# The shared expert's eight batches of a mixture-of-experts layer: next batch's tiles transposed earlier, the down product in two halves, scatters behind the subtractions, and 71 routed blocks in place of 72

## What is computed

```python
def _experts(x_flat, Wg, Wu, Wd):
    g = jax.nn.silu(jnp.einsum('nc,eci->nei', x_flat, Wg))
    u = jnp.einsum('nc,eci->nei', x_flat, Wu)
    return jnp.einsum('nei,eic->nec', g * u, Wd)

def _moe(x, Wgate, expert_bias, Wg, Wu, Wd, sWg, sWu, sWd):   # C = 512, E, K, I, S = 8, 2, 256, 1
    xf = x.reshape(-1, c)
    shared = jnp.mean(_experts(xf, sWg, sWu, sWd), axis=1)
    probs = jax.nn.softmax(xf @ Wgate + expert_bias, axis=-1)
    topk_p, topk_i = jax.lax.top_k(probs, K)
    topk_p = topk_p / jnp.sum(topk_p, axis=-1, keepdims=True)
    comb = jnp.sum(jax.nn.one_hot(topk_i, E, dtype=xf.dtype) * topk_p[..., None], axis=1)
    routed = jnp.einsum('ne,nec->nc', comb, _experts(xf, Wg, Wu, Wd))
    return (shared + routed).reshape(b, t, c)

# in the layer: xn = _rmsnorm(x, w_ln2); return x + _moe(xn, ...)
# around it:    x = x + tanh(g_ffn[0]) * layer(layernorm(x), ...)
```

## Time and profile before

| | us |
|---|---|
| median of 3 runs (lowest, highest) | 2361.26 (2359.19, 2361.65) |
| the profiled execution, its own time | 2359.61 |
| its span, first to last instruction | 2357.6 |
| start of the shared expert's first product on PE | 1792.18 |
| start of the routed stage's first block on PE | 2001.05 |

### The profile page before, as it was taken

The page is one execution under the profiler, slowest core; times in us unless marked ns, Lnnn a source line. Parts: engine busy times, 40 slices in busy tenths (PEclk is TensorE's granted clock), DMA queues, the critical chain, the costliest instruction groups (busy, mean ns, idle before and its releaser), DMA issues. The chain is left out here.

```text
span 2357.6 us, 43584 instructions
## 1 busy us (share of the span) xinstructions
PE 2130.3 (90%) x12672; PEld 972.2 (41%) x12673; DVE 1505.5 (64%) x4218; ACT 1177.9 (50%) x2316; POOL 1364.2 (58%) x1452
## 2 busy tenths in 40 slices
PE   3899999999999968899999999999976787999997
PEld 1333333333333313444444444444433343455554
DVE  3688888888888873656656656565535587344443
ACT  3355555555555543354545445454436473455553
POOL 3267767767767764265656565565451664455554
PEclk7999999999999978999999999999997898999999
DMA  5413323232332233453434435353314675666665
GB/s 172 156 56 107 95 90 108 77 113 70 107 104 76 85 101 94 139 151 95 141 119 134 129 96 161 89 155 120 102 50 118 132 179 106 110 112 113 115 108 88
DMA packets 222851, 263.78 MB, mean 112 GB/s; under 512 B 39192, under 2 KB 165004, under 8 KB 222388
## 3 DMA queue, kind: packets, MB, share of 16 engines
q1 hardware_dynamic: 197612, 212.79, 30.2%
q0 software_dynamic: 22976, 48.38, 11.9%
q10 hardware_dynamic: 2072, 0.28, 0.1%
HBM read 162.12 MB, written 86.80 MB: 106 GB/s over the span
## 5 line engine op out<-in xcount | busy, mean ns | idle before, releaser
L501 ACT ACTIVATE a_pt<-a_bank 128x512 f32<-128x512 f32 x512 | 305.6, 597 | 371.5 <-DVE a_bank L608 368.3
L1412 DVE CUSTOM_DVE_ANT_0 b_bank<-b_bank,b_tri 128x256 f32<-128x256 f32 (+3 forms) x512 | 253.6, 497 | 302.9 <-PE b_bank L1555 298.6
L619 DVE CUSTOM_DVE_ANT_0 a_bank<-a_bank,a_strip 128x512 f32<-128x512 f32 x512 | 353.1, 690 | 4.9 <-PE a_bank L762 4.3
L411 POOL TENSOR_TENSOR a_acc<-a_acc,a_pt 128x512 f32<-128x512 f32 x256 | 317.4, 1270 | 16.2 <-ACT a_pt L501 15.7
L1193 POOL TENSOR_TENSOR b_acc<-b_acc,b_pt 128x256 f32<-128x256 f32 (+2 forms) x384 | 270.9, 725 | 90.6 <-ACT b_pt L1284 71.3
L608 DVE TENSOR_TENSOR a_bank<-a_bank,a_band 128x256 f32<-128x256 f32 (+1 forms) x512 | 205.6, 402 | 129.6 <-PE a_bank L749 128.4
L1284 ACT ACTIVATE b_pt<-b_bank 128x256 f32<-128x256 f32 (+2 forms) x384 | 143.8, 383 | 190.9 <-PE b_bank L1539 181.0
L749 PE MATMUL a_bank<-a_q_stack,a_k_stack 128*128 128x512 f16 x512 | 199.3, 390 | 22.7 <-ACT a_pt L501 14.0
L762 PE MATMUL a_bank<-a_k_stack,a_q_stack 97*128 97x512 f16 x512 | 196.4, 384 | 4.6 <-DVE a_low L619 4.5
L1933 POOL DMA_INDIRECT out_dram<-c_z,c_to_row x72 | 114.1, 1585 | 138.7 <-DMA out_dram<-c_z,c_to_row 101.8
L408 POOL TENSOR_TENSOR a_acc<-a_pt 128x512 f32<-128x512 f32 x128 | 159.9, 1270 | 4.9 <-ACT a_pt L501 4.9
(11 more groups left out here) (346 smaller groups left out, 5432.3 us busy)
## 6 DMA issues: line engine op xcount, KB each, us to landing
b_q_stack<-qk_rows SPq DMA_DIRECT2D x192, 128.0 KB, 2.6
a_q_stack<-qk_rows SPq DMA_DIRECT2D x96, 128.0 KB
a_k_stack<-qk_rows SPq DMA_DIRECT2D x96, 128.0 KB
b_k_stack<-qk_rows SPq DMA_DIRECT2D x96, 128.0 KB, 2.6
a_sums<-in_x SPq DMA_DIRECT2D x34, 256.0 KB, 3.1
qk_rows<-a_qk_hi SPq DMA_DIRECT2D x64, 128.0 KB, 1.7
qk_rows<-a_qk_lo SPq DMA_DIRECT2D x64, 128.0 KB, 1.8
out_dram<-a_sums SPq DMA_DIRECT2D x32, 256.0 KB, 2.0
```

What stands on the lines that cost most here:

```text
L411: nc.gpsimd.tensor_tensor(acc[:, hh, :], acc[:, hh, :], mine, ALU.add).then_inc(pooled, 1)
L501: nc.scalar.activation(pt[:, n % SLOTS, :], st_bank[n % 2][:], ACT.Exp).then_inc(exped, 1)
L619: nc.vector.tensor_tensor_reduce(out=max_bank[step % 2][:], in0=max_bank[step % 2][:], in1=strip[:, g * HG + hh, at:at + S], scale=-1.0, s ...
L1412: nc.vector.tensor_tensor_reduce(out=max_bank[step % 2][:, 0:w], in0=max_bank[step % 2][:, 0:w], in1=tri[:, at:at + w], scale=-1.0, scalar ...
```

## The change

It has five parts.

1. The next batch's tiles are transposed in the first half of a batch (tiles 0 and 1 after the first of the four up products, 2 and 3 after the second), and the copies and subtractions that go with them move too. On ACT, `square(b + 2)` now stands between the two halves, ahead of `squash(b, 1)`, and `normalise(b + 2)` at the end of the batch.
2. The down product is done in two halves: for tiles 0 to 2 first half 0 of the contraction, then half 1, then tile 3 whole. The first half waits for the low part of hidden half 0 only.
3. On POOL the scatters are dealt out by an iterator over (batch, tile): they may lag by up to a batch, and fewer of them stand between the two subtractions. `rms(b + 2)` now stands ahead of the second subtraction. The buffers `place_i` and `record` and the semaphore `scattered` are threefold in place of twofold.
4. On DVE, `choose(b + 1)` comes ahead of the weights' last part, and in the last batch `lay_blocks` stands ahead of the second `activate`.
5. `NB` is 71 in place of 72 (the most blocks that the ceilings of eight counts with the sum 64 x 128 can need), so the loop has 15 turns and more blocks are written out behind it.

```diff
-NB = 2 * TT + E
+NB = 2 * TT + E - 1
...
-            for j in range(NB - 4, NB + 1):
+            for j in range(NB - 4 - NB % 4, NB + 1):
                 call(Count(0, j, 4))
...
+            tiles = iter(itertools.product(range(B), range(NT)))
+            left = [B * NT]
+
+            def scatter_some(b, n):
+                for _ in range(min(n, left[0] - (B - 1 - b) * NT)):
+                    scatter(*next(tiles))
+                    left[0] -= 1
...
                 if b > 1:
-                    scatter(b, (0,))
+                    scatter_some(b, 2)
                 low_part(b, 0)
-                if b == 1:
-                    scatter(0, (0, 1))
-                elif b:
-                    scatter(b, (1, 2))
-                low_part(b, 1)
-                if b == 1:
-                    scatter(0, (2, 3))
-                elif b:
-                    scatter(b, (3,))
+                if b > 1:
+                    scatter_some(b, 1)
                 if b + 2 < B:
                     rms(b + 2)
-                if b == 1:
-                    scatter(1, range(NT))
+                low_part(b, 1)
+                if b:
+                    scatter_some(b, 2 if b > 1 else NT)
...
                 squash(b, 0)
                 if more:
                     high(b + 1, 0)
                     high(b + 1, 1)
+                    scale_gate(b + 1, range(0, 2))
+                    high(b + 1, 2)
+                    high(b + 1, 3)
                 hidden_high(b, 0)
-                if more:
-                    scale_gate(b + 1, range(0, 2))
+                if b + 2 < B:
+                    square(b + 2)
                 squash(b, 1)
                 if more:
-                    high(b + 1, 2)
-                    high(b + 1, 3)
+                    scale_gate(b + 1, range(2, 4))
                 hidden_high(b, 1)
-                if more:
-                    scale_gate(b + 1, range(2, 4))
                 if b + 2 < B:
-                    square(b + 2)
+                    normalise(b + 2)
                 if more:
                     exponential(b + 1)
                 weights(b + 1)
...
-                activate(b, 0)
-                if not more:
-                    lay_starts()
-                    low_part(0)
                 if more:
                     low(b + 1, 0)
                     low(b + 1, 1)
+                else:
+                    lay_starts()
+                activate(b, 0)
+                if more:
+                    low(b + 1, 2)
+                    low(b + 1, 3)
+                else:
+                    low_part(0)
+                    lay_blocks()
                 if b:
                     up_weights(b)
                 activate(b, 1)
...
-                for t in range(NT):
-                    down(b, t)
+                for t in range(NT - 1):
+                    down(b, t, (0,))
+                for t in range(NT - 1):
+                    down(b, t, (1,))
+                down(b, NT - 1, (0, 1))
```

More of the change, by code:

```diff
@@ L1745, in pass_c @@
             sem(n) for n in ("logits_done", "routed", "expd", "chosen_set", "ranked", "placed", "weighed", "recorded"))
-        scattered = [sem(f"scattered{i}") for i in range(2)]
+        scattered = [sem(f"scattered{i}") for i in range(3)]
         ranks_read, spare_found, blank_set, blanked, table_ready = (
@@ L1823, in _, with enter @@
             sp.wait_ge(table_ready, 1)
-            for i in range(2):
-                sp.wait_ge(scattered[i], 16 * 2 * NT * (B // 2))
+            for i in range(3):
+                sp.wait_ge(scattered[i], 16 * 2 * NT * ((B - i + 2) // 3))
+            def enter(j, u, use):
+                sp.wait_ge(entered[u], use * 16 + 16)
+                sp.nop(nofuse=True)
+                at = sp.value_load(block_i[0:1, 1, bass.ds(j, 1)], min_val=0, max_val=E * CAP + (E - 1) * P)
+                sp.dma_start(entry[:, bass.ds(j, 1), :].rearrange("p a f -> p (a f)"), table[bass.ds(at, P), :]).then_inc(entered[u], 16)
             with sp.Fori(0, NB // 4) as i:
                 for u in range(4):
[L1828 to L1832, removed]
+                    enter(i * 4 + u, u, i)
+            for j in range(NB // 4 * 4, NB):
+                enter(j, j % 4, j // 4)
             for i in range(3):
@@ L1862, in write_records, with scatter @@
                                       ).then_inc(recorded, 1)
-            def scatter(b, tiles):
-                s = b % 2
-                if b == 0:
+            def scatter(b, t):
+                s = b % 3
+                if (b, t) == (0, 0):
                     pool.wait_ge(blanked, 32)
[L1868 to L1873, removed]
+                if t == 0:
+                    pool.wait_ge(weighed, b + 1)
+                    pool.wait_ge(recorded, 2 * b + 2)
+                for c in range(2):
+                    pool.indirect_dma_start(table, bass.IndirectOffsetOnAxis(place_i[:, s, t, c:c + 1], 0), record[:, s, t, c, :], None
+                                            ).then_inc(scattered[s], 16)
+            tiles = iter(itertools.product(range(B), range(NT)))
[4 more added lines that the diff above has]
+                    left[0] -= 1
             nc.gpsimd.memset(ones[:], 1.0).then_inc(const_set, 1)
@@ L2016, in _ @@
                 high(0, t)
+            square(1)
             scale_gate(0, range(NT))
-            square(1)
+            normalise(1)
             exponential(0)
@@ L2021, in _ @@
                 more = b + 1 < B
-                if more:
-                    normalise(b + 1)
                 squash(b, 0)
@@ L2297, in _ @@
                 if more:
-                    low(b + 1, 2)
-                    low(b + 1, 3)
+                    choose(b + 1)
                 if b:
                     down_weights(b)
-                if more:
-                    choose(b + 1)
-                else:
-                    lay_blocks()
                 for t in range(NT):
@@ L2406, in up, with down @@
                 last.then_inc(up_done, 1)
-            def down(b, t):
-                pe.wait_ge(h_lo_done, NI * b + NI)
+            def down(b, t, halves):
                 if t == 0 and b:
@@ L2412, in down @@
                 c = slice(t * P, (t + 1) * P)
-                for i in range(NI):
+                for i in halves:
+                    pe.wait_ge(h_lo_done, NI * b + i + 1)
                     mm(tile_bank[t][:], h_hi[:, i, c], d_hi[:, i, :], start=(i == 0), stop=False)
@@ L2416, in down @@
                     last = mm(tile_bank[t][:], h_lo[:, i, c], d_hi[:, i, :], start=False, stop=(i == NI - 1))
-                last.then_inc(downed, 1)
+                if NI - 1 in halves:
+                    last.then_inc(downed, 1)
             pe.wait_ge(const_loaded, 16 * 11)
@@ L2434, in _ @@
                     turn(b + 1, 1)
+                up(b, 0, 1)
+                if more:
+                    turn(b + 1, 2)
+                    turn(b + 1, 3)
                 up(b, 1, 0)
```

29 lines of the change are left out of this document (12 added, 17 removed).

## The result

| | before | after |
|---|---|---|
| median of 4 runs (lowest, highest), us | 2360.23 (2357.58, 2361.65) | 2385.91 (2382.63, 2392.71) |
| span of the profiled execution, us | 2357.6 | 2390.8 |
| mean granted clock over the span | 0.963 | 0.955 |

The changed kernel takes 1.0114 times as long (95% interval 1.009 to 1.0138), 25.7 us more by the medians.

What follows compares the result with a forecast made beforehand. The prediction took the shared expert to lose time by waits and a sinking clock, and the change to close a loop through z: 30.1 + 2.4 - 2.8 + 2.4 - 4.9 = +27.2 us, so 2387 us, range 2378 to 2396.

Steps and rivals of the forecast that it cites:

- The loop: Batches 2 to 5: store, load of z, squares, second half, next store close a loop, 29.96 us a batch, +30.1 us.
- The way from A to the squares: From POOL issuing a batch's accumulating DMA (A) to ACT's first square on the z loaded after it: mean 16.9 us.
- the prediction's sum: Batches 2 to 5: way, squares, tanh, high and low part, 15 matmuls (ten at the lower clock), next A: 29.96 us.
- ACT's idle time: Sign in batches 2 to 5: ACT idles some 10 us before each batch's squares, with the tanh behind them.
- That POOL's place alone would do it: Shared expert, POOL: second low part queued through rms ahead of it; no size given to this place alone.
- Batch 1: A(0) to A(1): POOL's scatters bind, squares come at 23.8 us as a small DMA stands between; 40.5 for 38.1, +2.4.
- Batch 6: Batch without squares: the first down half covers the low part, 19.6 us in place of 22.4, -2.8.
- The last batch: lay_blocks, 4.93 us on DVE, moves ahead of the second gated product and PE waits; finish_rows through at 25.8 us, +2.4.
- One block less: Routed stage: one block and one turn of the loop go, -4.9 us.
- The sum: All terms together: 30.1 + 2.4 - 2.8 + 2.4 - 4.9 = +27.2 us.
- Lighter traffic: Rival: way of 15.4 us to the squares, clock recovers, POOL's scatters bind at 27.1 us a batch; 2375 us, chance 0.09.
- Faster: Rival: z does not gate, PE binds batches at 19.6 us, -16.5 us in all; 2343 us, chance 0.08.

Runs made afterwards that it cites:

- e1: Changed kernel with a fourth buffer for z, all else the same: 2343.54 us, 0.991 of the kernel before.
- e4: Kernel before with one added wait, ACT waiting for the load of z of batch b+2 ahead of its second tanh; nothing moved: 2395.91 us, 1.0135.
- e9: As e3, but normalise ahead of the weights on ACT and rms ahead of the scatters on POOL: 2370.65 us, 1.0031 of the kernel before.
- e2: Changed kernel with ACT's squares put back behind the second high part, normalise behind the weights, POOL as changed: 2387.92 us, 1.0104 of the kernel before.
- e3: As e2, and on POOL rms behind the second low part and its scatters as well: 2350.69 us, 0.9941 of the kernel before.
- e5: Changed kernel with lay_blocks put back behind the last batch's second gated product on DVE, one run: 2390.04 us.
- e6: Changed kernel with 72 routed blocks again, one run: 356.64 us from the first routed product to the end, against 352.29 with 71.
- e7: Changed kernel with each batch's store as a plain DMA, without accumulation onto the output: 2358.91 us, 0.9985 of the kernel before.
- e8: Changed kernel with fourth z buffer, its load before the first batch, lay_blocks put back, two scatters for four in batch 1: 2326.86 us, 0.9844 of before.

## Why the prediction was right

- **The loop** closed as forecast: 121.5 us for four batches against 119.8. The way from A to the squares, the disputed term, was 18.43, 16.20, 16.05 and 17.27 us; their mean, 17.0, is the 16.9 taken from before. e1 to e4 show that it is the load of `z` and the place of its waits, and not the down product in halves or the dealt scatters.
- **The spread within the loop** was not forecast. Of the 15 matmuls not ten but 14, seven, twelve and twelve ran at the lower level in batches 2 to 5. With these counts (0.21 us more or less for each) and each batch's own way the prediction's sum gives 32.3, 28.6, 29.5 and 30.8 us; measured were 32.34, 28.71, 29.64 and 30.79. So the two terms carry the whole spread, and one mean for all four was good enough for the sum.
- **ACT's idle time** before the squares was 15.01, 8.82, 8.66 and 9.90 us (forecast: some 10), PE's between the halves 14.55, 8.35, 8.20 and 9.44 (some 8), and the stage's clock 0.84 (below 0.9). The waits of batch 2 are longer because A(1) came late: POOL was still scattering, and PE was already 5.0 us into batch 2 (from 1858.64) when it was issued, in place of 1.05.
- **The loop was not quite open before.** The prediction has it that the squares need not be there until the batch ends, and so no loop. But on POOL `rms(b + 2)` stood straight ahead of A(b), and in batch 2 that was the path; the kernel before, on POOL:

```profile
1878.80 0.19 POOL L1843 TENSOR_SCALAR c_mean<-c_squares 128x4 f32<-128x4 f32 x1 [5.66 <-ACT c_xn L1969]
...
1880.10 1.42 POOL L1849 DMA_DIRECT2D out_dram<-c_z  x1
```

  From A(1), 18.45 us to the square, 2.67 to `rms` and 1.30 to A(2) are the 22.42 us of that batch. DVE's last sum had ended at 1878.55 (1877.80 and 0.75), so A(2) went out some 1.5 us later than DVE allowed; A(3) to A(5) waited for DVE. The forecast took its 89.7 us from the rows and was not touched by this, but e9's loop is this one with four scatters added.
- **That POOL's place alone would do it** the prediction said only in passing ("on POOL, through `rms` ahead of it"). e2 makes it a cause of equal rank. Undoing ACT's move alone would have brought nothing.
- **Batch 1** is the step that failed: +2.4 forecast, -1.8 found. The chain was right (POOL still binds, and A(1) has no idle time ahead of it), but the way was 19.7 us, not 23.8. SP issued the load 13.8 us after A(0), as against 14.9, and the square followed 5.9 us after it, as against 8.9. The next two points say what stands behind these two parts.
- **Why batch 1's store was late.** The reason given for 23.8 was wrong as well. The small DMA went out 0.9 us after A(0) (1828.26) and held up nothing in the queue: the load was issued when the store landed, 13.8 us after A(0), where the stores A(1) to A(4) took 9.4 to 11.0. Why this store took longer no run shows; the small DMA was under way beside it.
- **Why batch 1's load was short.** Before, the load of the down weights went out 3.4 us behind it, and after, 14.1 us. But in e2, e3 and e9 it went out 3.3 to 4.0 us behind and the load still took 5.4 to 6.0 us, so the weights are not the cause. What else differs is POOL's scatters: before, they ran beside the load from its start (1832.97 on), and after, POOL stood still until 1849.66. In e4, with scatters from the start and the weights late, the load took 7.8 us, and in e3, where the first scatter came 2.0 us behind it, 5.5. No run moved the scatters alone.
- **Batch 6** without squares took 19.66 us (19.6 forecast), and PE waited 0.71 us for the second low part, with the clock at full speed.
- **The last batch** cost the 2.4 us forecast; `finish_rows` was through 25.85 us into it (from 2003.63 to 2029.48), where the prediction said 25.8. e5 gives 2.7.
- **One block less** gave 4.3 us in place of 4.9, and 4.35 in e6; the difference is within what the stretch varies.
- **The sum** is better than its terms. Inside the stage and behind it +26.1 was found for +27.2, but batch 1 came out 4.2 us lower and the other terms together 3.1 us higher. That the median lies within 1.1 us of the forecast is in part luck.
- **The rivals.** Lighter traffic: the way shortened in two batches to 16.20 and 16.05 us but never to 15.4, and the clock did not recover. Faster: e1 shows the 19.5 us batches that it rested on, and they needed a fourth buffer. At e7's way of 12.7 us the prediction's sum for a batch gives 12.7 + 13.1 = 25.8 us, and 25.7 was measured. That e7 as a whole is even with before (the prediction struck the balance at 10.1 us) comes from batch 1, 6.1 us below before, and from the routed stage's 7.2 us.

## What to carry to other kernels

An in-order engine passes its wait on to all that stands behind it. Before a step is moved ahead, find out what it waits for, and if that hangs on the end of an earlier batch, add up the way round: with `z` in three buffers it was 30 us beside a batch with 19.5 us of work, and a fourth buffer turned a loss of 1.1% into a gain of 0.9%. Look at every engine on which the moved data are awaited, since undoing one of two such places gives nothing back (e2), and a repair can close another loop, through other work that stands in the same queue (e9).

## What was not expected of the hardware

- An accumulating store of 1 MB held SP's next load back for 10.1 us (mean of four), a plain one of the same bytes from the same queue for 6.0. The issue itself took POOL 1.42 and 0.83 us.
- The same plain load of `z` took 15.8 us when it was issued 1.4 us after an accumulating store (e1, batch 1), and 6.9 (mean of four) when it was issued after the store had landed. That store took longer too, 15.9 us to its landing in place of 13.8 (the same store in the changed kernel). The small DMA into the table ran beside both, so its share is not parted from theirs; in e7, issued 5.0 us after the plain store and with the small DMA beside it, the load took 10.3 us.
- A PE that had waited some 8 us ran its next matmuls at 0.43 us each, but how many varied between nearly equal waits: seven after 8.35 us, 12 after 8.20, 14 after 8.16 (e2). In the changed kernel and e1, after waits of 0.45 to 0.82 us, and once after 2.27 (e1, batch 2), they stayed at 0.21; after 2.00 (e8, last batch) eight ran at the lower level. In the kernel before seven did after 0.91 us (1895.04, batch 3), with a wait of 2.22 us shortly ahead of it. So the length of the last wait does not tell the number; what does, the runs leave open.
- The two passes ahead of the stage vary by 7 us between executions of the same instructions (first shared product at 1792.15 to 1799.23 us). A single profiled span is thus no measure for a change of a few microseconds; distances inside the stage are.
